# Reordering the reloads and the first output tile at the end of a selective scan (decoder layer, one core)

## What is computed

```python
xz = x @ W_in + b_in
x_proj, z = jnp.split(xz, 2, axis=-1)          # 1024 each
x_conv = silu(x_proj)
B, C = jnp.split(x_conv @ W_xproj + b_xproj, 2, axis=-1)   # 16 states
dt = softplus(x_conv @ W_dt + b_dt)
# scan over time, per channel and state:
h = h * exp(dt * A) + (dt * u) * B;  y_t = sum_s(h * C) + D * u
y = y * silu(z)
x = layernorm(x + (y @ W_out + b_out))
```

## Time and profile before

| | |
|---|---|
| time, median of 3 runs | 3070.46 us (3069.9 to 3070.63) |
| the profiled execution | 3076.67 us, its span 3074.9 us |
| busy: TensorE / VectorE | 2829.6 us (92%) / 2667.3 us (87%) |
| busy: ScalarE / GpSimd | 2031.6 us (66%) / 1889.5 us (61%) |
| mean granted TensorE clock | 0.985 of full |

### The profile page before, as it was taken

How to read it: one execution, slowest core, us unless ns; L and a number is a source line. 1 busy time by engine, 2 the same in 40 slices (tenths; PEclk the granted TensorE clock), 3 DMA queues, 4 the chain that set the end, 5 groups by cost and what they waited for, 6 DMA issues and landing times. The chain is left out here.

```text
span 3074.9 us, 49084 instructions
## 1 busy us (share of the span) xinstructions
PE 2829.6 (92%) x18958; PEld 1266.6 (41%) x18958; DVE 2667.3 (87%) x3018; ACT 2031.6 (66%) x3654; POOL 1889.5 (61%) x992
## 2 busy tenths in 40 slices
PE   7988989889889889889889898999999999999998
PEld 2222222222222222222222223566666767677675
DVE  5999999999999999999999898766666777777775
ACT  6776776786777777777777645555555566556564
POOL 4898998999999999989989886411111111121100
PEclk9999999999999999999999999899999999999999
DMA  4111112112121121121112334501111000010000
GB/s 164 52 49 53 59 48 73 52 36 73 52 64 49 48 66 60 35 66 60 40 61 80 94 110 139 196 32 49 52 43 40 23 23 23 24 37 30 24 8 15
DMA packets 123897, 176.65 MB, mean 57 GB/s; under 512 B 15154, under 2 KB 50610, under 8 KB 123156
## 3 DMA queue, kind: packets, MB, share of 16 engines
q1 hardware_dynamic: 123668, 173.51, 17.6%
HBM read 104.33 MB, written 67.04 MB: 56 GB/s over the span
## 5 line engine op out<-in xcount | busy, mean ns | idle before, releaser
L918 POOL TENSOR_TENSOR h<-h,c_rep 128x1024 f32<-128x1024 f32 x511 | 1197.1, 2359 | 151.4 <-ACT carry L659 150.8
L809 DVE TENSOR_TENSOR_SCAN h<-r_ps,carry,h 128x512 f32<-128x512 f32 x768 | 937.9, 1260 | 4.3 <-ACT r_ps L653 4.0
L653 ACT ACTIVATE r_ps<-r_ps,decay 128x512 f32<-128x512 f32 x1024 | 633.3, 658 | 298.8 <-PE r_ps L403 298.4
L796 DVE TENSOR_TENSOR h<-u_ps,b_rep 128x1024 f32<-128x1024 f32 x512 | 611.6, 1194 | 19.0 <-PE u_ps L416 18.8
L416 PE MATMUL u_ps<-dtu,spread 32*128 32x512 f16 x2048 | 313.6, 383 | 92.9 <-DVE h L796 90.0
L403 PE MATMUL r_ps<-dt,spread 32*128 32x512 f16 x2048 | 313.8, 382 | 40.8 <-DVE h L809 40.4
L1999 POOL TENSOR_TENSOR o_in<-o_in,rows 128x1024 f32<-128x1024 f32 x15 | 36.9, 2461 | 490.2 <-DMA o_in<-o_dram 490.2
L809 DVE TENSOR_TENSOR_SCAN h<-r_ps,zero,h 128x512 f32<-128x512 f32 x256 | 312.9, 1262 | 10.4 <-ACT r_ps L653 10.2
L433 PE MATMUL y_ps<-h,gather 128*32 128x512 f32 x2048 | 279.4, 612 | 9.5 <-ACT uz L664 8.7
L40 PE MATMUL fps<-x,region 128*128 128x256 f16 x1024 | 281.2, 275 | 3.1 <-issue 2.4
L41 PE MATMUL fps<-x,region 128*128 128x256 f16 x1024 | 280.7, 274 | 0.0
(11 more groups left out here) (259 smaller groups left out, 5671.1 us busy)
## 6 DMA issues: line engine op xcount, KB each, us to landing
u_t_dram<-u SPq DMA_DIRECT2D x16, 1024.0 KB, 5.3
uz<-u_t_dram SPq DMA_DIRECT2D x64, 256.0 KB, 3.9
z_t_dram<-zs SPq DMA_DIRECT2D x32, 512.0 KB, 3.4
uz<-z_t_dram SPq DMA_DIRECT2D x64, 256.0 KB, 3.9
y_t_dram<-uz SPq DMA_DIRECT2D x64, 256.0 KB, 2.1
region<-y_t_dram SPq DMA_DIRECT2D x32, 256.0 KB, 3.5
result<-x SPq DMA_DIRECT2D x16, 512.0 KB, 2.8
x_t<-dram_x_t SPq DMA_DIRECT2D x15, 512.0 KB, 4.7
```

The lines of the kernel that those rows point to most:

```text
L653: nc.scalar.activation(bank, bank, ACT.Exp, scale=decay[:, col:col + 1]).then_inc(s_da, 1)
L796: nc.vector.tensor_tensor(h[:, g % H_GROUPS, o:o + 2, :], u_ps[:, :, :], b_rep[:, c % 2:c % 2 + 1, :].broadcast_to([P, 2, TS]), ALU.mult). ...
L809: nc.vector.tensor_tensor_scan(row, r_ps[:, 2 * (pair % 2) + o, :], row, start, ALU.mult, ALU.add)\
L918: nc.gpsimd.tensor_tensor(rows, rows, c_rep[:, c % 2:c % 2 + 1, :].broadcast_to([P, 2, TS]), ALU.mult)\
```

## The change

Three things, all in the last chunk. The reloads of y tiles 0 to 3 stand at s = 18, 19, 20 and 21 in SyncE's order (before 19, 22, 25, 28), ahead of the attention part's loads at s = 22. Tile 0's pieces stand at pairs 23, 24 and 25 (before 24, 25, 26), and with them its high half (pair 21) and low halves (21 and 22); keep-awake matmuls remain at pairs 21 and 22 only. Its sum with x on VectorE stays at pair 26, one behind its last piece.

```diff
 class OutTile:
     def __init__(self, i):
-        at = OUT_AT + i // 2 * 5 + i % 2 * 3
+        at = OUT_AT + i // 2 * 5 + i % 2 * 3 - (1 if i == 0 else 0)
...
                 for i in range(OUT_TILES):
-                    if s == OUTS[i].first - (5 if i < 2 else 4):
+                    if s == (W_OUT_AT + 3 + i if i < 4 else OUTS[i].first - 4):
                         load_y_tile(i)
...
-                if PLANS[-1].dt[-1][-1] - PAIRS < s < OUT_AT:
+                if PLANS[-1].dt[-1][-1] - PAIRS < s < OUTS[0].first:
...
-                if s == OUTS[0].last:
+                if s == OUTS[0].last + 1:
                     x0_tile(0)
```

## The result

The changed kernel takes 3074.98 us, the kernel before, in 20 runs beside it, 3072.06. The ratio is 1.0012, 95% interval 1.0006 to 1.0017: slower by 3.7 us, between 1.8 and 5.2 (the two medians alone are 2.9 apart). The forecast was +2.0 us and "within 0.2%". The kernel before was itself 1.6 us slower in these 20 runs than in the three of the profile before (3070.46), so the change and not the absolute time is what to compare. Time differences here are as small as the scatter of single runs (before: 3064.6 to 3077.8), so most of what follows rests on distances inside the traces (the two profiled executions even go the other way, 3075.65 us changed against 3076.67).

- **D**, from the first low half of w_out on VectorE (L820, pair 17, ahead of everything that is changed) to the second sum with x (L827, pair 28).

A forecast was written before the change was run, and what follows sets the result against it. VectorE, busy 99.6 of 100 us, was taken to bound the kernel. Tile 0's move gains 3.37 us, a new stall costs 3.2, the x0 wait and queue the rest: +2.0 on 3070.46, so 3072.5 us, range 3067.5 to 3076.5.

The forecast's parts named there:

- The reload wait of ScalarE goes and nobody is ready to use it: ScalarE, high half of y tile 1: the 1.94 us DMA wait goes, but that half starts only at 1756.9 instead of 1754.75.
- TensorE gets the input 2.3 us sooner, not a pair sooner: TensorE, tile 0's first piece: GpSimd's low half starts at 1740.81 instead of 1743.12, so the piece begins at 1742.11.
- A new stall at the product for pair 26 in place of the one at the first sum: VectorE, dB*u product: a new 3.2 us stall takes the place of the 3.37 us wait at the first residual sum.
- the clock paragraph: TensorE: clock low at about 1742 for some 3.4 us, costing 1.7 us on the pieces, hidden under the x0 wait.
- The bias waits for x0 until 1752.98: TensorE, bias matmul in tile 0's last piece: ready at 1750.8, it waits for the x0 load at most until 1752.98.
- no effect: Rival, 13%: x0 lands by 1750.8 and the clock stays high; only 0.2 us are left, 3070.7 us.
- The spread of dt 27 at 1755.1, tile 1's low half at 1757.9: TensorE's spread behind the waiting bias at about 1755.1; GpSimd's low half starts at about 1757.9 instead of 1755.88, 2.0 us later.
- Second sum at 1768.6, +2.0: VectorE, residual sum of tile 1: tile 1's pieces, sums and bias follow as before, 2.0 us later, at about 1768.6.
- It carries over whole to the end: From the second residual sum on the order is the old one, so the 2.0 us shift carries over whole: 3072.5 us.
- one long low stretch: TensorE's clock low for 6.8 us once instead of 3.4: +4 us, given as the upper reach of the range.
- the waits really go: Rival, 12%: TensorE gets tile 0's input when it asks, no new stall; 5.4 us gained, 3065.1 us.
- The clock stays low twice: Rival, 7%: two long low stretches of TensorE's clock, at 1742 and at tile 1's pieces; +8.3 us, 3078.8 us.

The follow-up runs named there:

- x0 first alone: Changed kernel with the loads of b_out and x0 issued first at pair 22, ahead of the two weights and the context; ratio to the kernel before 1.0006.
- both freed: Changed kernel with b_out and x0 loaded first and 14 keep-awake matmuls at pair 23 instead of none; ratio to the kernel before 1.0006.
- the keep-awake kernel: Changed kernel with the six keep-awake matmuls of pair 23 put back ahead of tile 0's first piece; ratio to the kernel before 1.0009.
- all three obstacles gone: Changed kernel with GpSimd's first low half ahead of dt7's dt*u, b_out and x0 loaded first, keep-awake matmuls at pair 23; ratio to the kernel before 1.0004.
- GpSimd's order alone: Changed kernel with GpSimd's first low half of y tile 0 ahead of dt and dt*u of dt7 at pair 21; ratio to the kernel before 1.0022.

## Why the prediction was right

The mechanism came as forecast up to the second sum. That the shift then carries over whole is not shown, and one premise about x0 was wrong without mattering; both are said below. The steps in order, each against the trace of the changed kernel (whose start is 0.06 us later on the clock):

- *The reload wait of ScalarE goes and nobody is ready to use it.* Right: the high half of tile 1 began at 1756.85 with no wait (1756.9 said), and the reloads alone were worth 0.40 of D.
- *TensorE gets the input 2.3 us sooner, not a pair sooner.* Right: first piece at 1742.15 (1742.11 said), behind a wait of 3.48.
- *A new stall at the product for pair 26 in place of the one at the first sum.* Right, and the clock decided its size: 3.2 was the row-by-row value, 4.9 that with the clock low; it was 4.71. That is a hit for the clock paragraph, not for the 3.2 that the sum uses. The clock fell behind the idle stretch, as forecast; the keep-awake matmuls that stood there were cover. But six of them are no sure cover: of the four kernels that had them back at pair 23, one still had the clock low at the first piece.
- *The bias waits for x0 until 1752.98.* Right: 1753.00. The lower bound (1750.8) fell away, and with it the rival "no effect". But its premise, three reloads queued behind x0, didn't hold in the kernel before: only that of tile 1 (0.5 MB) was issued right behind x0, tiles 2 and 3 not before 1750.78, when x0 had 2.2 us to go (rows in the last section).
- *The spread of dt 27 at 1755.1, tile 1's low half at 1757.9.* Right: 1755.05 and 1757.98. Both paths to it, over x0 and over the late carry, are equally long: the high half of tile 1 ended at 1757.9 (1756.85 and 1.05 long), GpSimd was free at 1757.98. With x0 first alone D didn't move, and with both freed it fell.
- *Second sum at 1768.6, +2.0.* 1769.05, +2.4 in D. The last piece of the sum was the weakest: I moved tile 1's whole block by 2.0, though its low-clock part isn't bound to it; the first piece of tile 1 took 4.37 us (1759.28 to 1763.65) instead of 3.96. The kernel before had 4.37 too when it was profiled again, so this 0.4 is chance and the forecast +2.0 fits the 1.98 against that profile.
- *It carries over whole to the end.* Not shown. The time says +3.7 (1.8 to 5.2), the trace +2.0 to +2.4 at pair 28, which agrees, but at the end of the scan phase E has only +0.7 or +1.1 left, by which profile of the kernel before is taken. That the time came out at 3074.98, 2.5 above the forecast 3072.5, is to 1.6 us the kernel before's own difference between its runs. It lies within the range, but the upper end of 3076.5 is not "one long low stretch": at the stated +4 that reaches 3074.5 only.

The rival "the waits really go" was right in kind, it needs TensorE to get its input when it asks, but its price was too high. (Its "8.3 us" should be 8.1, the two waits; and its 0.7 us isn't derived from the 1.2 it names.) The kernel that gave TensorE the input (low half ahead of dt7's work, x0 first, keep-awake) shortened D by 2.4, not by 5.4, and 1.28 of that is the clock at tile 1: GpSimd's queue sets when tile 1 can start, and it remains. "The clock stays low twice" didn't come: in the changed kernel the low stretches at 1743 and 1760 were about 3.4 us each. That longer ones occur was shown by the keep-awake kernel, where it stayed low from 1754 to 1764.

## What to carry to other kernels

When work is moved a step sooner on an engine that goes strictly in order, the question isn't whether its own input will be there one step sooner but who stands behind it in that queue: here the scan's spreads of dt stood behind a piece and behind a bias, and each wait of the piece became a wait of the engine that bounds the kernel. Put the input's maker in order first (GpSimd's low half ahead of work that is needed later, the one small load ahead of the large ones), and only then move the consumer. Ask first, though, whether the input's maker has room: here GpSimd had no gap, and even with all three obstacles gone tile 1's input came no sooner than with the reloads alone. Removing one of two equally long paths shows nothing. And a reordering can delay something else: GpSimd's order alone put the issue of x0 back by 2.9 us, and that kernel stood 0.22% above before (0.13 to 0.32), the changed one 0.12% (0.06 to 0.17).

## What the runs showed of the hardware

- **Loads ahead of a load delay it; whether loads behind it do is hardly tried here.** In the kernel before, SyncE issued x0 and what follows it so:

```profile
1744.21 0.37 SPq L361 DMA_DIRECT2D region<-dram_x  x1
1744.63 2.40 SPq L342 DMA_DIRECT2D region<-y_t_dram  x2
...
1750.78 3.57 SPq L342 DMA_DIRECT2D region<-y_t_dram  x4
```

  x0 was usable at 1752.98, 8.8 us after its issue, with the reload of tile 1 (0.5 MB) right behind it. In the changed kernel it was usable at 1753.00, 9.1 us after its issue at 1743.91, without that reload, but with two other loads (0.5 MB together) right behind it instead. Moved ahead of the 2.3 MB, in the kernel with all three obstacles gone, it was there before TensorE asked, 7.1 us after its issue (1739.79 to 1746.86), so it took at least 1.7 us less.
- **One and the same operation, the low half of two blocks of w_out, took 2.94, 2.10, 1.19 and 1.19 us** on VectorE (L820, pairs 17 to 20 of the changed kernel), and the first came back as 2.94 to 3.07 in every run. Where it was longest, GpSimd was in its multiplication (1711.13 to 1713.49), and GpSimd's next operation then took 2.14 instead of 1.16 us. Where it took 1.19 beside GpSimd's dt*u (1723.61, L900), that one took 2.24 instead of 1.26:

```profile
1711.13 2.36 POOL L918 TENSOR_TENSOR h<-h,c_rep 128x1024 f32<-128x1024 f32 x1 [1.52 <-ACT carry L659]
1713.45 2.14 POOL L905 TENSOR_TENSOR dt<-dt 128x512 f16<-128x512 f32 x1
```

  The two seem to exclude each other there. No run tried it alone, so it is a reading of the rows. The Trainium skill, GPSIMD Engine Reference, section Specifications, says that GpSimd's SBUF interfaces are shared with VectorE, with contention when VectorE's instruction has two SBUF inputs, as this one has; the rows agree.
- **Where the clock falls differs between executions of one kernel**, and by it single waits of VectorE: 2.03 or 0.33 us at the same product. The first piece of tile 1 took 2.68 us in one kernel and 4.32 in another whose program is the same up to there, with the granted clock at 1.00 and at 0.56 to 0.58. One profile of each kernel isn't enough to compare anything below 2 us.
